# Two turns of the tensor engine and one copy of the scalar engine moved, where an attention block meets the next layer's rows

## What is computed

```python
x = x + _L1_xattn_ref(_layernorm(x, axis=-1), ctx_4096, L1_xattn_Wq, ..., L1_xattn_k_norm_w)
x = x + _L1_ffn_ref(_layernorm(x, axis=-1), L1_ffn_weight, L1_ffn_bias)
x = x + _L2_xattn_ref(_layernorm(x, axis=-1), ctx_4096, ctx_4096, L2_xattn_Wq, ..., L2_xattn_Wo)
```

## Time and profile before

| what | value |
|---|---|
| median of 3 runs | 1564.63 us (1563.31 to 1567.21) |
| profiled execution, its own time | 1561.94 us |
| its span, first to last instruction | 1560.1 us |
| TensorE clock granted, mean | 0.990 of full |
| PE busy | 1481.5 us, 95% of the span |
| DVE, ACT, POOL busy | 818.8, 749.4, 440.0 us |
| the stretch around the change | about 925 to 1030 us |

### The profile page before, as it was taken

How to read it: one execution, slowest core, us unless ns; L and a number is a source line. 1 busy time by engine, 2 the same in 40 slices (tenths; PEclk the granted TensorE clock), 3 DMA queues, 4 the chain that set the end, 5 groups by cost and what they waited for, 6 DMA issues and landing times. The chain is left out here.

```text
span 1560.1 us, 32993 instructions
## 1 busy us (share of the span) xinstructions
PE 1481.5 (95%) x13148; PEld 1224.1 (78%) x13154; DVE 818.8 (52%) x1681; ACT 749.4 (48%) x2560; POOL 440.0 (28%) x557
## 2 busy tenths in 40 slices
PE   6999979999999999999999998879999999999998
PEld 4777767889898888988888887656656778888876
DVE  3778865544444545544443457776665421343365
ACT  4656554445555444554544565365443212455451
POOL 1364433222212222121222224354222000123433
PEclk9999999999999999999999999999999999999999
DMA  8000010110100001010000110010100001122201
GB/s 254 18 11 17 4 43 27 62 42 28 41 28 28 20 22 42 28 42 28 28 25 17 41 55 1 30 56 1 41 1 1 26 6 57 49 76 72 53 20 62
DMA packets 44537, 58.62 MB, mean 38 GB/s; under 512 B 25520, under 2 KB 32704, under 8 KB 41568
## 3 DMA queue, kind: packets, MB, share of 16 engines
q1 hardware_dynamic: 43872, 56.05, 11.5%
q10 hardware_dynamic: 448, 0.46, 0.1%
q0 software_dynamic: 64, 0.00, 0.0%
HBM read 48.89 MB, written 2.10 MB: 33 GB/s over the span
## 5 line engine op out<-in xcount | busy, mean ns | idle before, releaser
L1882 ACT ACTIVATE big<-pb 128x128 f32<-128x128 f32 x384 | 106.6, 278 | 299.7 <-PE pb L922 196.4
L2221 POOL TENSOR_TENSOR big<-big 128x512 f32<-128x512 f32 x96 | 100.0, 1042 | 259.5 <-DVE big L1513 259.5
L1931 ACT ACTIVATE big<-pb,big 128x128 f32<-128x128 f32 x384 | 136.0, 367 | 57.5 <-issue 34.0
L1508 DVE TENSOR_REDUCE big<-pb 128x4 f32<-128x512 f32 x96 | 65.8, 686 | 177.7 <-PE pb L961 170.0
L937 PE MATMUL pb<-wkh,CXh 128*128 128x256 f32 x512 | 149.8, 292 | 0.0
L937 PE MATMUL pb<-wkl,CXh 128*128 128x256 f32 x512 | 145.0, 283 | 0.0
L937 PE MATMUL pb<-wkh,CXl 128*128 128x256 f32 x512 | 144.3, 282 | 0.0
L2211 POOL TENSOR_SCALAR big<-big 128x6 f32<-128x6 f32 x64 | 12.9, 202 | 413.7 <-ACT big L1882 413.1
L1300 DVE TENSOR_TENSOR X<-X,pb 128x512 f32<-128x512 f32 x128 | 86.8, 678 | 75.5 <-PE pb L1148 39.3
L988 PE MATMUL pb<-woh,oh 128*128 128x512 f32 x256 | 113.0, 442 | 0.0
L922 PE MATMUL pb<-wqh,CXh 128*128 128x512 f32 x256 | 101.8, 398 | 3.0 <-DVE big L1478 1.6
(11 more groups left out here) (279 smaller groups left out, 3781.6 us busy)
## 6 DMA issues: line engine op xcount, KB each, us to landing
big<-in_w SPq DMA_DIRECT2D x17, 1024.0 KB, 4.9
big<-in_w SPq DMA_DIRECT2D x24, 256.0 KB, 3.0
big<-in_w SPq DMA_DIRECT2D x8, 512.0 KB, 3.6
o<-o SPq DMA_DIRECT2D x96, 32.0 KB, 1.9
X<-in_x SPq DMA_DIRECT2D x8, 256.0 KB, 5.0
big<-in_cn SPq DMA_DIRECT2D x8, 256.0 KB, 2.7
CXlf<-in_cT SPq DMA_DIRECT2D x8, 256.0 KB, 5.0
big<-in_wa SPq DMA_DIRECT2D x1, 2048.0 KB, 7.7
```

Of the source, the lines that this page charges most:

```text
L1508: v.tensor_reduce(m[j % 2], quarters(bank(p)), AX, MAX, negate=True).then_inc(S.m, 1)
L1882: y = a.activation(sq[i % 2], bank(p)[:, j * width:j * width + 128], ACT.Square, accum_out=ss[i % 2][:, first + j:first + j + 1])
L1931: y = a.activation(e_[:, c], bank(p)[:, c], ACT.Exp, bias=m[j % 2][:, k:k + 1], scale=1.0, accum_out=z[j % 2][:, k:k + 1])
L2221: g.tensor_tensor(quarters(e_), quarters(e_), bc(r[j % 2], 128), MUL).then_inc(*on.to(S.pn))
```

## The change

Three things in ORDER, and a new name for an old function. First, l2_turn t for t = 0 to 4 is taken from its place behind f1_mm and put directly behind l1_d (59 + t). Second, the work that f1_turn named on two engines gets two names: f1_turn is now PE's turn alone, f1_copy is ACT's copy alone. Third, for t = 0 to 3, f1_turn leaves its place behind l1_k and is put directly behind l1_s (60 + t), and f1_copy directly ahead of l1_s (60 + t); for t = 4 to 7 both stay together where f1_turn was.

For step 62 the list after reads: l1_q 62, l1_b 61, l1_t 60, l1_k 62, f1_norm 2, l2_rows 0, f1_copy 1, l1_s 61, f1_turn 1, l1_n 62, l1_z 61, l1_v 60, f1_mm 1, f1_quant 2, l1_d 59, l2_turn 0, f1_stats 3, l2_stats 1.

```diff
@@ -232,6 +232,18 @@
             k, k_u = k + 1, k_u + 1
         order.insert(k_u, ("f0_ints_u", t))
         order.insert(k, ("f0_ints", t))
+
+    for t in range(5):
+        order.remove(("l2_turn", t))
+        order.insert(order.index(("l1_d", 59 + t)) + 1, ("l2_turn", t))
+
+    for t in range(NT):
+        k = order.index(("f1_turn", t))
+        if t < 4:
+            order.pop(k)
+            k = order.index(("l1_s", 60 + t))
+            order.insert(k + 1, ("f1_turn", t))
+        order.insert(k if t < 4 else k + 1, ("f1_copy", t))
     return order
...
-            def f1_turn(t):
+            def f1_copy(t):
                 if t >= 2:
                     w = PSUM["f1_mm", t - 2, "p"]
                     on.wait_ge(w.full, w.n + 1)
...
-                      l1_b=l1_b, l1_s=l1_s, l1_t=l1_t, l1_v=l1_v, l1_d=l1_d, f1_turn=f1_turn, l2_kv=l2_kv,
+                      l1_b=l1_b, l1_s=l1_s, l1_t=l1_t, l1_v=l1_v, l1_d=l1_d, f1_copy=f1_copy, l2_kv=l2_kv,
```

## The result

The changed kernel has a median of 1566.88 us (22 runs, 1564.64 to 1570.34), beside 1563.49 us for the kernel before (22 runs on the same chips, 1559.72 to 1567.21). The ratio is 1.0023, with a 95% interval of 1.0015 to 1.0030: 3.4 to 3.6 us slower, where +2.5 us was forecast. This lies within the 0.3% that were taken as no change, though the interval leaves 1 out.

A forecast was written before the change was run, and what follows sets the result against it. The tensor engine bounds the kernel, while the DVE-POOL ring paces these steps. +0.9 us from the moved stages and +1.6 us from the clock gave +2.5 us on a 1564.6 us median: 1567.1 us, range 1563.0 to 1570.5.

The forecast's parts named there:

- The round over DVE and POOL: Steps 61 to 64: DVE to POOL and back sets the pace, 14.0 us a step; PE's waits are slack beside it.
- (b): f1_turn on PE behind the scores: four transposes, 0.4 us each time as before; waits of 0.91 and 0.15 us go.
- (c): ACT's copy behind f1_norm and l2_rows: PE's wait only changes its name; the ring lengthens, about +1.5 us on DVE by step 64.
- the ring: The loop DVE to POOL and back to DVE, with ACT in it almost without slack, pacing the steps at 14.0 us.
- (d): The way out: the projection fills the wait ahead of l2_turn 4, but l2_turn 5 comes 0.9 us late, carried to the end.
- the 0.6 us that is taken in: At l2_turn 5: ACT began l2_rows 5 about 0.6 us behind POOL, which absorbs that much of the lateness.
- (e): PE's clock: pauses ahead of f1_mm 0, f1_mm 3 and l2_turn 5 bring half clock; bounds 0 to 4.5 us, taken as 1.6.
- partly hidden by the ring: Clock drops at the first and second pauses of PE are partly covered by DVE's pace; one at the third is not.
- the drops of the kernel before are nearly free: Half-clock stretches behind PE's waits of 2.03 and 2.93 us cost almost nothing, since DVE's ring was behind.
- The first: Rival: the projections hide the waits for rows at the five moved places, up to -10.8 us, 1553.8 us; chance 6%.
- The second: Rival: clock drops in steps 61 to 64 and ahead of l2_turn 5 make PE's round decide, +6.9 us, 1571.5 us; 17%.
- The third: Rival: seam loss is partly slack at the start of l2, 0 to +1 us, 1565 us; counted within the 77% no-change case.

The follow-up runs named there:

- rows_turn_only: Kernel before with only the five l2_turn put behind the projections, turn and copy of f1 where they were: 1563.63 us, ratio 0.9997.
- shorter_ring: Kernel before with l2_turn behind the projections, f1_norm and l2_rows behind the cast of l1_v, POOL's root ahead of the statistics: 1560.03 us, ratio 0.9972.
- copy_before_norm: The whole change, but with the copy ahead of f1_norm of the same step: 1562.40 us, ratio 0.9986 to the kernel before.
- after_again: The changed kernel itself, same file, measured again in a second set on one chip: 1566.95 us, ratio 1.0022 to the kernel before.
- after_filled: Changed kernel plus 11 unused matmuls in each pause ahead of f1_mm 0, f1_mm 3 and l2_turn 5: 1559.88 us, ratio 0.9980 to the kernel before.
- before_filled: Kernel before plus unused matmuls, 7 ahead of l2_turn 2 and 10 ahead of l2_turn 4: 1559.43 us, ratio 0.9975.

## Why the prediction was right, and where its steps were not

The direction and the cause in its outline came out, and the size roughly: +2.5 us was forecast, 3.4 to 3.6 us were measured. That the forecast time, 1567.1 us, is only 0.2 us off is in part luck. It started from a median of three runs, 1564.6 us, that lies 1.1 us above the median of 22, and this makes up for a change sized about 1 us too small. Two terms were mis-sized, in opposite directions.

- **The round over DVE and POOL sets the pace.** Right. rows_turn_only took PE's waits at the moved places away and gained nothing; shorter_ring has PE's order from rows_turn_only, took 1 us a step out of the round, and gained.
- **(b), the turn behind the scores, is harmless.** Right, by copy_before_norm, which has it and doesn't lose.
- **(c), the copy behind l2_rows turns the wait into another.** Right, and its size too: line 1022's wait was forecast at about 10 us and is 10.2 (12.3 in after_again), line 767's under 2 and is 1.7, line 750's about 5 and is 5.4.
- **(c), the ring grows by 1.5 us until step 64.** This term was too large. The changed kernel's own profile shows 1.4 us, which looks like a hit, but 1.0 us of it came at one stroke, in step 62, when DVE waited 2.21 us for PE's scores behind a slow stretch. In after_again and after_filled, where f1_mm 0 was followed by none, it is 0.4 to 0.5 us. What I had missed: the first third of a microsecond makes DVE's next instruction shorter by as much. The integer mask of the rounding (line 1333) took 1.16 us in step 61 because POOL adds the bias to X at the same time:

```profile
940.88 1.16 DVE L1333 TENSOR_SCALAR big<-xn 128x512 int32<-128x512 int32 x1
```

  In the changed kernel it starts 0.36 us later against the same stretch and takes 0.77 us (the row at 942.20 above): 0.39 us come back. In both kernels the mask ends about 0.28 us behind POOL's addition (941.75 and 942.69), whenever it starts. So DVE is back on its old times there in each step, and the lateness doesn't add up: in after_again the low parts of steps 61, 62 and 63 are each 0.33 us late against step 60.
- **(d), l2_turn 5 comes 0.9 us late.** It came at 1019.02 - 0.96 - 1015.36 = 2.7 us late. The mechanism was right (the 2.93 us ahead of l2_turn 4 went, a new pause of 2.98 us came, where about 3.5 was forecast), and so was the 0.6 us that is taken in: what arrives at l2_turn 5 is the lateness of the low part of l1_v 63 less 0.65 us, in the changed kernel (3.4 and 2.7), in after_again (1.3 and 0.7) and in after_filled (0.3 late and 0.3 early). The shift was mis-sized, not the way it takes. With the pauses filled l2_turn 5 isn't late at all, where +0.9 us was in the sum.
- **(e), the clock, 1.6 us.** Too small: about 2.7 us by the comparison above (3.4 to 3.6 us of loss without the filling, 0.8 us with it), though the intervals allow anything up to 5.5 us, and 3.8 to 4.8 us by the seams of the profiles (151.9 and 152.9 against 148.1 us). The places were right, 3 of 3 in the first profile and 2 of 3 in after_again, and a fourth was missed ahead of l2_turn 7. What failed is the step "partly hidden by the ring": behind f1_mm 3 the ring gives no cover, since l1_v 63, whose cast DVE needs next, stands behind the projection, two l2_kv and a turn on PE. There 1.4 us of lateness grew to 3.4 (in after_again 0.5 grew to 1.3, in after_filled, without the drop, 0.4 became 0.3). That the drops of the kernel before are nearly free was right for the first, by the time of l2_turn 3 in before_filled; for the second it is open.
  The rule of the Trainium skill that was weighed there ("TensorE: Matmul & The Clock Gate", "HAM oscillation — how this bites in real kernels") would have given +5.4 us. The runs lie between: in the first profile each of the three pauses did bring a slow stretch, as it says, in after_again the first, of 3.18 us, did not, and cover took a part of what I priced.
- **The rivals.** The first, -10.8 us, fell with rows_turn_only and the whole change. The second, +6.9 us, had the right mechanism at the two ends, and not in steps 62 and 63, where the pauses were 1.0 us (1.8 and 1.3 us in after_again), as was said against it. The third, that nothing reaches the end, is wrong: the medians differ by 3.4 us.

## What to carry to other kernels

Before a wait is moved behind other work, ask what the work in front of it now waits for: here a copy that had stood in idle time went behind the very instruction that the moved turn had waited for, and the wait kept its length under another name. A wait on the bounding engine that another engine's round paces is slack; shorten the round (a root ahead of the statistics, norms behind the cast) and the slack turns into time. And price a pause of the tensor engine at its length and at the slow matmuls behind it: whether these cost anything is decided by what stands behind them in the queue.

## What the runs showed of the hardware that I had not expected

**A wait far away moved with the length of the program.** The wait for the repacking DMA near 1536 us is 1.6 to 2.4 us in the nine profiles without added matmuls, and 0.5 us or none in the five with 11 to 33 of them, 500 us earlier. The queues of the kernel before, in the stretch from 1531 to 1537 us, hold one packet of the instruction queue q8 beside the repacking (packets, MB, share of 16 engines):

```profile
q1 hardware_dynamic: 240, 0.10, 6.6%
q8 instruction: 1, 0.02, 1.7%
```
